# Delta layer, output part: u times k kept in its PSUM bank, q times the states moved to GpSimd, VectorE's loop written out

## What is computed

```
def step(S, inp):
    qt, kt, vt, at, bt = inp
    Sk = einsum('bhde,bhe->bhd', S, kt)
    S_new = at * S - at * bt * outer(Sk, kt) + bt * outer(vt, kt)
    ot = einsum('bhd,bhde->bhe', qt, S_new)
    return S_new, ot
x = x + (O.reshape(b, n, c) @ Wo.T + bo)
```

## Time and profile before

| what | value |
|---|---|
| three executions, median | 1973.47 us |
| profiled execution, its time | 1971.24 us |
| profiled execution, its span | 1969.5 us |
| share of the span busy: TensorE, VectorE, ScalarE, GpSimd | 67%, 77%, 47%, 13% |
| the block `delta_out` | about 1561 to 1743 us of the span |

### The profile page before, as it was taken

The page is one execution under the profiler, slowest core; times in us unless marked ns, Lnnn a source line. Parts: engine busy times, 40 slices in busy tenths (PEclk is TensorE's granted clock), DMA queues, the critical chain, the costliest instruction groups (busy, mean ns, idle before and its releaser), DMA issues. The chain is left out here.

```text
span 1969.5 us, 42398 instructions
## 1 busy us (share of the span) xinstructions
PE 1324.6 (67%) x15088; PEld 718.6 (36%) x15088; DVE 1517.7 (77%) x2925; ACT 918.3 (47%) x2025; POOL 253.8 (13%) x298
## 2 busy tenths in 40 slices
PE   4689999999999999941999580000000188822998
PEld 2215555554555555340666250000000033421665
DVE  5698999899989998071665676999999799971665
ACT  4508888888888888950443560002222100030443
POOL 6000000000000000025045000000000000034044
PEclk9859999999999999975999675555555599965999
DMA  3611111111111100032243229311212100012243
GB/s 90 175 42 27 32 30 30 30 30 30 42 45 30 30 3 3 2 111 58 53 68 50 79 104 161 111 43 43 57 46 60 54 0 0 0 52 58 56 67 44
DMA packets 118652, 100.85 MB, mean 51 GB/s; under 512 B 23665, under 2 KB 100018, under 8 KB 118066
## 3 DMA queue, kind: packets, MB, share of 16 engines
q1 hardware_dynamic: 101570, 84.79, 16.8%
q0 software_dynamic: 11264, 8.92, 3.1%
q10 hardware_dynamic: 5616, 4.47, 1.4%
HBM read 55.98 MB, written 31.21 MB: 44 GB/s over the span
## 5 line engine op out<-in xcount | busy, mean ns | idle before, releaser
L727 DVE TENSOR_REDUCE att_negmax<-att_ps_max 128x1 f32<-128x1024 f32 x512 | 620.9, 1223 | 66.0 <-PE att_ps_max L590 37.3
L715 ACT ACTIVATE att_probs<-att_ps_prob 128x512 f32<-128x512 f32 x1024 | 556.3, 595 | 128.7 <-PE att_ps_prob L605 126.5
L590 PE MATMUL att_ps_max<-av_k_op,av_q_op 81*32 81x512 bf16 x4096 | 417.9, 401 | 13.2 <-PEq L104 7.2
L605 PE MATMUL att_ps_prob<-av_q_op,av_k_op 99*32 99x512 bf16 x4096 | 407.2, 382 | 2.7
L625 PE MATMUL att_ps_acc<-att_probs,att_vq 128*32 128x256 f32 x4096 | 313.4, 379 | 0.0
L1935 PE MATMUL out_ps_y<-all_bo_row,all_ones 1*128 1x128 f32 x2 | 0.8, 481 | 373.2 <-PEq L104 373.2
L590 PEld LDWEIGHTS att_ps_max<-av_k_op,av_q_op 81*32 81x32 bf16 x4096 | 111.9, 97 | 146.5 <-DVE att_negmax L727 44.9
L605 PEld LDWEIGHTS att_ps_prob<-av_q_op,av_k_op 99*32 99x32 bf16 x4096 | 108.7, 95 | 146.1 <-ACT att_probs L715 94.3
L625 PEld LDWEIGHTS att_ps_acc<-att_probs,att_vq 128*32 128x32 f32 x4096 | 130.3, 111 | 78.4 <-issue 0.5
L1154 ACT ACTIVATE moe_moe_gate<-moe_moe_ps_h 128x256 f32<-128x256 f32 x122 | 46.8, 383 | 214.4 <-PE moe_moe_ps_h L1095 201.3
L1935 PEld LDWEIGHTS out_ps_y<-all_bo_row,all_ones 1*128 1x128 f32 x2 | 0.5, 308 | 373.4 <-issue 373.4
(11 more groups left out here) (277 smaller groups left out, 2038.1 us busy)
## 6 DMA issues: line engine op xcount, KB each, us to landing
moe_moe_xin<-expert_rows SPq DMA_DIRECT2D x182, 72.0 KB
av_k_op<-terms_k SPq DMA_DIRECT2D x48, 216.0 KB
av_q_op<-terms_q SPq DMA_DIRECT2D x144, 72.0 KB
solve_dec_and_windows<-solve_Xw SPq DMA_DIRECT2D x16, 256.0 KB, 3.0
solve_dec_and_windows<-solve_k SPq DMA_DIRECT2D x16, 256.0 KB, 3.7
terms_q<-qkv_parts_q SPq DMA_DIRECT2D x8, 384.0 KB, 2.6
terms_k<-qkv_parts_k SPq DMA_DIRECT2D x8, 384.0 KB, 3.1
all_w_all<-in_f_w SPq DMA_DIRECT2D x24, 128.0 KB, 2.5
```

The source lines that it names most:

```text
L590: mm = pe.matmul(ps_max[c * STRIP:(c + 1) * STRIP, a % 2, k * CH:(k + 1) * CH], q_op[s][0:R_ALL, h, at:at + STRIP], k_op[s][0:R_ALL, h, k ...
L605: mm = pe.matmul(ps_prob[c * STRIP:(c + 1) * STRIP, j % 2, :], k_op[s][0:R_END, h, at:at + STRIP], q_op[s][0:R_END, h, half * CH:(half + 1 ...
L715: act.activation(probs[:, j % PROBS, :], ps_prob[:, j % 2, :], ACT.Exp).then_inc(s_exp, 1)
L727: dve.tensor_reduce(negmax[:, s % 2, a:a + 1], ps_max[:, a % 2, :], AX.X, ALU.max, negate=True).then_inc(s_maxed, 1)
```

## The change

VectorE's product of u and k is written back over k in the same PSUM tensor, and the buffer `kd` is gone. The scan reads its second operand from PSUM. The product q times St goes to GpSimd, which waits for each scan and, from the third step on, for the `sum_o` that read the same qS buffer two steps before. The scan waits for GpSimd to have read the St buffer of two steps before. TensorE may refill `ps_k` for step n only when the scan of step n - 2 has read it. VectorE's loop over sequences is straight code for all four, and u times k of step e + 1 no longer goes ahead of anything: it stands between two scans.

```
-        kd = m.sb("kd", [P, 2, S])
...
+            for b in range(B):
+                for e in range(D):
+                    n = D * b + e
+                    pool.wait_ge(s_S, n + 1)
+                    wait_used(pool, s_o, n - 1)
+                    pool.tensor_tensor(qS[:, e % 2, :], q[:, b * S:(b + 1) * S], St[:, e % 2, :],
+                                       ALU.mult).then_inc(s_qS, 1)
+
...
-                wait_used(pe, s_kd, n - 1)
+                wait_used(pe, s_S, n - 1)
...
-                dve.tensor_tensor(kd[:, e % 2, :], u[:, bass.ds(b * S, S)], ps_k[e % 2][:, :],
+                dve.tensor_tensor(ps_k[e % 2][:, :], u[:, b * S:(b + 1) * S], ps_k[e % 2][:, :],
                                   ALU.mult).then_inc(s_kd, 1)
...
-            def body(b):
-                tok = bass.ds(b * S, S)
-                spread_u(b, 0)
+            for b in range(B):
+                tok = slice(b * S, (b + 1) * S)
                 for e in range(D):
                     n = D * b + e
+                    spread_u(b, e)
                     dve.wait_ge(s_kd, n + 1)
-                    dve.tensor_tensor_scan(St[:, e % 2, :], a[:, tok], kd[:, e % 2, :], 0.0, ALU.mult,
+                    wait_used(dve, s_qS, n - 1)
+                    dve.tensor_tensor_scan(St[:, e % 2, :], a[:, tok], ps_k[e % 2][:, :], 0.0, ALU.mult,
                                            ALU.add).then_inc(s_S, 1)
-                    if e < D - 1:
-                        spread_u(b, e + 1)
-                    dve.wait_ge(s_S, n + 1)
-                    wait_used(dve, s_o, n - 1)
-                    dve.tensor_tensor(qS[:, e % 2, :], q[:, tok], St[:, e % 2, :], ALU.mult).then_inc(s_qS, 1)
-                    if e == 3 and not (isinstance(b, int) and b == 0):
+                    if e == 3 and b:
                         add(b - 1)
-            repeat(dve, B, body)
             add(B - 1)
```

## The result

| | before | changed |
|---|---|---|
| median of four executions | 1972.95 us | 1948.11 us (1945.02 to 1950.08) |
| ratio, 95% interval | | 0.9876 [0.9855, 0.9896] |
| profiled span | 1969.5 us | 1946.9 us |

The change makes the kernel 24.8 us faster; 1948 us was forecast. Timed once more, beside the last experiment, the ratio was 0.9871 [0.9856, 0.9886].

What follows compares the result with a forecast made beforehand. VectorE was taken as the bound, with TensorE close behind. Terms of -31.4 + 6.1 + 1.0 = -24.3 us took the span from 1969.5 to 1946.9 us and the median to 1949.2 us; forecast 1948 us, range 1942 to 1960 us.

Steps and rivals of the forecast that it cites:

- VectorE's beat: In the 32 steps, VectorE's time per step falls from 4.45 to 3.47 us, a gain of 31.4 us.
- The pair at the start of the block: First u times k and the scan right behind it in the old trace: 1.26 + 2.21 = 3.47 us.
- PSUM operands at nothing: VectorE's scan reading PSUM and u times k writing it were taken to cost no extra time.
- rival of a write at half rate: VectorE's u times k into PSUM takes 2.28 us, making the kernel 1976 us; chance 4 in 100.
- GpSimd's product: On GpSimd, q times St takes 2.20 us, within the 3.47 us step.
- rivals that needed a product of 3.34 us or over 4.4 us: On GpSimd, slower products: weaker gain, 1951 to 1963 us, 15 in 100; no gain, 1972 us, 3 in 100.
- TensorE's follow-up work: In the steps, project and route on TensorE make VectorE wait 6.1 us in all for ps_k.
- The slack: In a plain step, TensorE has 0.9 us in hand before VectorE asks for ps_k.
- The end: At the block's end, the uncovered last q times St takes 2.20 in place of 1.23 us, 1.0 us more.
- The clock: TensorE's granted clock could fall behind the three adds, costing up to 5 us; no fall was expected.
- The slower rival: VectorE and GpSimd shut each other out of SBUF in the steps, giving 2012 us; chance 8 in 100.
- The break-even of 0.98 us a step: In the steps, VectorE held up by GpSimd for 0.98 us, 45% of the product, decides the slower rival.

Runs made afterwards that it cites:

- the last experiment: The change with the product in halves and the statistics moved to behind the scan of step 7, beside the change: 1938.63 us, ratio to before 0.9836.
- e2: The kernel before with u times k written to PSUM and scanned from there, all products still on VectorE: 1972.36 us, ratio to before 0.9998.
- e7: The changed kernel with GpSimd's product in two halves of 512 tokens, each with its own semaphore count: 1943.78 us, ratio to before 0.9857.
- e5: The changed kernel with a 0.95 us GpSimd memset ahead of each product: 1950.06 us, ratio to before 0.9895.
- e4: The changed kernel with route computed for only the first 128 tokens of each sequence: 1944.0 us in one execution.
- e6: The changed kernel with each sequence's layer-norm statistics moved from behind the add to behind the scan of step 7: 1941.34 us, ratio to before 0.9852.
- e1: The changed kernel with u times k written to SBUF again, product still on GpSimd: 1972.4 us, ratio to before 0.9997.

## Why the prediction was right, point by point

**VectorE's beat.** Predicted 3.47 us a step, measured 3.44 us; the gain is 32 x (4.45 - 3.44) = 32.3 us in place of 31.4. The pair at the start of the block, from which the beat was taken, was a fair sample, for the waits between neighbours are in it.

**PSUM operands at nothing.** Right. e2 has the two of them alone, at +12 and -3 ns. By the fixed costs of the Trainium skill (VectorE - DVE Perf Modes, the TRN2 errata) the estimate was a scan 65 ns slower; the measurement decides against it. The rival of a write at half rate is ruled out by the same rows.

**GpSimd's product.** Predicted 2.20 us, measured 2.36 us. The two sizes of e7 and the change give (2355 - 1272) / 512 = 2.12 ns an element and 0.19 us fixed, where 1.99 and 0.16 were estimated. It hides behind VectorE's 3.44 us. So the rivals that needed a product of 3.34 us or over 4.4 us are out.

**TensorE's follow-up work.** Predicted 6.1 us of waits, measured 6.7, at the five places named. The slack was taken as 0.9 us and is 0.6: the longer product makes up 0.16 us of it, and `sum_o` starts another 0.15 us behind the product's end (1594.96 against 1592.46 + 2.35), which the prediction had at nothing. e5 showed that the product's delay passes into the waits, e4 that `route`'s work makes up 3.0 us of them, e6 that VectorE's work in the place of a wait removes it. `project`'s work was never taken out; its part is read from where the other waits stand. One detail was too strong: the wait behind `project` in sequences 2 and 3 was to be the whole 1.8 us, and is 1.65.

**The end.** Predicted 1.0 us; with the last product at 2.35 in place of 1.23 us, 1.1 us by the same working. The sum of the measured terms is -32.3 + 6.7 + 1.1 = -24.5 us, and the block shrank by 24.5 us. That both agree to a tenth is luck: a beat read wrongly by 0.01 us moves the sum by 0.3 us, and the faster last `route` gave 0.3 us that no term has. It was also some luck that the predicted sum of -24.3 us fell so close, for the beat gave 0.9 us more than forecast and the other two terms cost 0.7 us more. The working led to 1949.2 us and the forecast said 1948 us without a reason for the difference; that this met the median of 1948.11 us is chance, within executions from 1945.02 to 1950.08 us.

**The clock.** Predicted not to fall behind the threaded `add`s, and it did not: 1.00 in each slice there, where the kernel before had 0.66 (1675 to 1680 us). The prediction said nothing of the end of the block, where the clock was low before the change (0.50) and after it (0.64).

**The slower rival.** Its mechanism exists, as e1 shows, and what keeps it off is that the scan reads PSUM. There the prediction had only a rule of the Trainium skill (SBUF - State Buffer, "Who interferes with whom") that no run had shown; now e1 (3.44 us with two SBUF operands) and the changed kernel (2.29 us with one) show both sides of it. Its price was too high: it took the full 2.20 us of a product, while only the part beside a two-operand instruction counts. u times k runs free for the first 1.1 us, and 1.14 us a step are lost. The break-even of 0.98 us a step, 31.4 us in all, was about right: with 1.14 us in 28 of 32 steps, 31.9 us, e1 lands on the time of before.

## What to carry to other kernels

Moving work from a leading engine to an idle one pays only as far as the two don't shut each other out: in e1 that cost 1.14 us a step where the move had gained 1.01 us. In float32 code like this, where GpSimd multiplies two tensors from SBUF, VectorE's instructions beside it should take no more than one operand from SBUF. PSUM was a nearly free place for the other (12 ns a step in e2), at the price of a buffer that comes free one instruction later.

When the move brings the leader down to the follower's pace, price the follower's extra work in lumps against its slack, for what is left of the gain is decided there. Placing extra work of the two engines side by side is then worth as much as removing some of it: the moved statistics (e6) took 2.9 us off the waits, and leaving out most of `route` (e4) took 3.0 us. It also pays to put the leader's work where the leader waits at the end of a block, which gave e6 another 1.6 us.

## What was not expected of the hardware

In e1, VectorE's scan shut out by GpSimd shows no idle time. It appears as 3.44 us of busy time where 2.29 us are work, so that VectorE's share of busy time rises while its work stays the same. Only a comparison with the same instruction alone, as behind the `add`, told it here.
